# Second cross attention masked by TensorE, large stacks issued from ScalarE's queue, a new order of the streams

## The reference

```python
scores = einsum('bhqd,bhkd->bhqk', q, k) / sqrt(8)
scores = where(mask == 0, 1e-09, scores)      # X1; X0 has -inf here
attn = softmax(scores, axis=-1)
out = einsum('bhqk,bhkd->bhqd', attn, v)
return out @ WO_w.T + WO_b
```

## Time and profile before

| | |
|---|---|
| median of 3 runs | 1360.46 us (1351.87 to 1361.56) |
| profiled execution | 1365.99 us, span 1364.3 us |
| mean granted TensorE clock | 0.892 of full speed |
| busy: PE, DVE, ACT, POOL | 83%, 59%, 45%, 25% of the span |
| DMA | 58.01 MB, mean 43 GB/s |
| X1 of the lanes, round 1 | about 260 to 346 us |
| X1 of the lanes, round 2 | about 902 to 988 us |

### The profile page before, as it was taken

How to read it: one execution, slowest core, us unless ns; L and a number is a source line. 1 busy time by engine, 2 the same in 40 slices (tenths; PEclk the granted TensorE clock), 3 DMA queues, 4 the chain that set the end, 5 groups by cost and what they waited for, 6 DMA issues and landing times.

```text
span 1364.3 us, 19868 instructions
## 1 busy us (share of the span) xinstructions
PE 1133.4 (83%) x7245; PEld 648.8 (48%) x7320; DVE 811.5 (59%) x2073; ACT 618.7 (45%) x1068; POOL 342.7 (25%) x733
## 2 busy tenths in 40 slices
PE   6949567878689999969997866877869999978996
PEld 5934321443344577734465332233334467754454
DVE  3854789677873411477436379978687332169444
ACT  2116159435057543316732445844416753323852
POOL 3132210334334100124403121034334400032520
PEclk9769679779689899989978787988889999999988
DMA  7040000220600000150023200022150000042011
GB/s 251 1 109 14 0 1 1 64 55 24 172 9 2 3 0 1 45 143 3 3 62 84 54 11 0 1 55 55 57 138 3 4 1 1 1 124 65 2 34 45
DMA packets 48647, 58.01 MB, mean 43 GB/s; under 512 B 16637, under 2 KB 41645, under 8 KB 48046
## 3 DMA queue, kind: packets, MB, share of 16 engines
q1 hardware_dynamic: 47686, 56.26, 15.5%
q10 hardware_dynamic: 864, 0.48, 0.1%
HBM read 35.27 MB, written 20.87 MB: 41 GB/s over the span
## 4 chain that ended last, share of the span: by engine, by line
PE 58%; DVE 21%; issue 5%; DMA 5%; ACT 5%; POOL 4%; SPq 1%; ACTq 0%; POOLq 0%; DVEq 0%; another core or an unknown queue 0%
PE banks L1648 11%; PE banks L1658 9%; PE banks L1463 5%; PE banks L1451 5%; DVE sb_rmax L1593 4%; PE banks L1438 3%; DVE sb_arena L1383 2%; DMA sb_qs<-sb_mrows 2%; DVE sb_arena L1378 2%; PE banks L964 2%; PE banks L475 2%; PE banks L470 2%; PE banks L1264 1%; PE banks L680 1%; PE banks L1295 1%
## 5 line engine op out<-in xcount | busy, mean ns | idle before, releaser
L1593 DVE TENSOR_REDUCE sb_rmax<-banks 128x1 f32<-128x384 f32 (+3 forms) x352 | 206.5, 638 | 84.2 <-PE banks L1440 82.9
L1522 ACT ACTIVATE sb_arena<-banks 128x512 f32<-128x512 f32 x320 | 174.1, 599 | 106.0 <-PE banks L1451 82.9
L1438 PE MATMUL banks<-sb_arena,sb_qs 128*128 128x384 bf16 (+3 forms) x492 | 124.1, 324 | 42.5 <-DMA sb_arena<-k_scratch 19.3
L465 POOL TENSOR_SCALAR sb_var<-sb_mv 128x4 f32<-128x4 f32 x40 | 12.5, 311 | 570.1 <-DVE sb_mv L450 570.1
L1658 PEld LDWEIGHTS banks<-sb_w,sb_arena 128*128 128x128 f32 x1024 | 128.0, 192 | 39.9 <-issue 38.0
L1713 ACT ACTIVATE sb_arena<-banks,sb_b 128x512 f32<-128x512 f32 x128 | 84.2, 686 | 130.3 <-PE banks L1648 130.0
L1772 DVE SCALAR_TENSOR_TENSOR sb_xall<-banks,sb_region,sb_xall 128x128 f32<-128x128 f32 x160 | 44.5, 344 | 164.3 <-PE banks L1658 164.2
L1551 POOL TENSOR_SCALAR_AFFINE_SELECT sb_arena<-sb_arena 128x256 f32<-128x256 f32 x256 | 98.3, 409 | 168.0 <-ACT sb_arena L1522 167.7
L1319 ACT ACTIVATE sb_arena<-banks,sb_negmax 128x512 f32<-128x512 f32 x192 | 115.2, 714 | 42.4 <-PE banks L1264 28.3
L1648 PE MATMUL banks<-sb_ft,sb_w 128*128 128x512 f32 x256 | 129.6, 609 | 0.0
L1658 PE MATMUL banks<-sb_w,sb_arena 128*128 128x128 f32 x1024 | 129.2, 275 | 0.2 <-ACT sb_arena L1713 0.2
(11 more groups left out here) (286 smaller groups left out, 1937.8 us busy)
## 6 DMA issues: line engine op xcount, KB each, us to landing
sb_qs<-q_scratch SPq DMA_DIRECT2D x32, 288.0 KB, 5.0
q_scratch<-sb_region SPq DMA_DIRECT2D x16, 384.0 KB, 2.6
sb_arena<-k_scratch SPq DMA_DIRECT2D x16, 288.0 KB, 6.9
sb_arena<-in_chosen SPq DMA_DIRECT2D x8, 514.0 KB, 4.3
sb_w<-in_w SPq DMA_DIRECT2D x2, 2048.0 KB
q_scratch<-sb_region SPq DMA_DIRECT2D x16, 256.0 KB, 2.5
sb_qs<-q_scratch SPq DMA_DIRECT2D x32, 96.0 KB, 2.5
k_scratch<-sb_region SPq DMA_DIRECT2D x8, 384.0 KB, 2.7
```

The source lines that it names most:

```text
L1438: nc.tensor.matmul(o[:, i * kl:(i + 1) * kl], L.qs[:, h // 2, t * 128:kl], L.ks[:, key_of(h), 0:kl], start=(i == 0), stop=False)
L1522: nc.scalar.activation(L.probs[:, u % SLOTS, :], bank_of(SELF_ORDER, ring, ("key", u)), ACT.Exp)\
L1593: nc.vector.tensor_reduce(L.rmax[:, t, g * GROUP + h0:g * GROUP + h0 + nh], bank_of(SELF_ORDER, ring, ("max", step))[:, 0:nh * kl] .rearra ...
```

## The change

Four things are done.

1. X1's key scores are formed as in X0: the maximum's rows are copied into the stacked queries by SyncE (4 DMAs per X1, 16 in all, not issued before), a matmul with the identity adds -1e30 at masked keys (`shutt`), a second adds the scores. Masked keys so get weight 0. L1132 and L953 go.
2. Their share is added back at the end. TensorE sums, per query, the values (with their column of ones) of its masked keys: four fp32 matmuls per X1, of 144 columns each. VectorE copies the sums to `shut`. When all maxima are known GpSimd forms min(-max, 0) + 1e-9, ScalarE takes its exp, and GpSimd multiplies `shut` by it. `finish_tensor` adds `shut` to the spread sums by a matmul with the identity, 288 columns fp32, twice per X1.
3. The conversions of the mask (`cbias`, `maskt`, `mask`) move from X1's GpSimd stream into BU's. `shutt` is made in X1.
4. The "rest" stacks are issued from ScalarE's stream, in X0 and X1 (queries) and in S0 and S1 (queries and keys), in a piece right after the activation of queries (and keys) and before the step loop. The `ORDER` strings of all five engines are new.

```diff
-CROSS_KEY = (13, 9)
-CROSS_EXP = (13, 11)
+CROSS_KEY = (13, 13)
+CROSS_EXP = (13, 13)
...
 # cross_sync
             stack(sp, L, p, "q", L.qd, L.qs, slice(0, FIRST), "first")
-            stack(sp, L, p, "q", L.qd, L.qs, slice(FIRST, H // 2), "rest")
-            if j == 0:
-                for step in range(CROSS_STEPS):
+            for step in range(CROSS_STEPS):
...
 # cross_tensor: key_scores(h)
-                if j == 0:
-                    if h % GROUP == 0:
-                        pe.wait_ge(*p.at("mstacked", 16 * (h // GROUP + 1)))
-                    nc.tensor.matmul(o, identb[0:K2, :], L.cbiast, start=True, stop=False)
...
-            def less_maximum(h):
                 if h % GROUP == 0:
-                    pe.wait_ge(*p.at("mrows", h // GROUP + 1))
-                pe.wait_ge(*p.at("masked", h + 1))
-                nc.tensor.matmul(bank_of(order, ring, ("key", h)),
-                                 mselb[:, h % GROUP:h % GROUP + 1].to_broadcast([128, 128]),
-                                 L.mrows[:, h // GROUP % 2, :], start=False, stop=True, skip_group_check=True)\
+                    pe.wait_ge(*p.at("mstacked", 16 * (h // GROUP + 1)))
+                nc.tensor.matmul(o, identb[0:K2, :], L.shutt if j else L.cbiast, start=True, stop=False)
+                nc.tensor.matmul(o, keys_of(L, h), L.qs[:, h // 2, :], start=False, stop=True)\
                     .then_inc(L.sem("key"), 1)
...
+            if j:
+                yield
+                pe.wait_ge(*p.at("values", 1))
+                pe.wait_ge(*p.at("masks", 0))
+                for t in range(T):
+                    i = nc.tensor.matmul((b0, b3)[t // 2][:, t % 2 * H * OW:(t % 2 + 1) * H * OW],
+                                         L.maskt[:, t * 128:(t + 1) * 128], L.cvalues[:, OW:(H + 1) * OW],
+                                         start=True, stop=True)
+                i.then_inc(L.sem("summed"), 1)
 # finish_tensor, in X1
+                    if shut and two == 0:
+                        pe.wait_ge(*p.at("shut_sums", 1))
+                        nc.tensor.matmul(ring[pair][:, 0:2 * H * OW], ident[:], L.shut[:, 2 * pair:2 * pair + 2, :],
+                                         start=True, stop=False, skip_group_check=True)
 # cross_scalar
+            stack(act, L, p, "q", L.qd, L.qs, slice(FIRST, H // 2), "rest")
             for step in range(CROSS_STEPS):
...
+                if j and step == G * T + 4:
+                    yield
+                    act.wait_ge(*p.at("cut", 1))
+                    nc.scalar.activation(L.rmax[:], L.rmax[:], ACT.Exp).then_inc(L.sem("shut_exp"), 1)
 # cross_pool
-                nc.gpsimd.tensor_scalar(L.cbias[:], L.mask1, 0.0, -BIG, ALU.is_equal, ALU.mult)
-                nc.gpsimd.tensor_scalar(L.maskt[:], L.mask1t, 0.0, 0.5, ALU.is_equal, ALU.is_lt)
-                nc.gpsimd.tensor_scalar(L.mask[:], L.mask1, 0.0, None, ALU.is_equal).then_inc(L.sem("masks"), 1)
+                nc.gpsimd.tensor_scalar(L.shutt, L.maskt[:], -BIG, None, ALU.mult).then_inc(L.sem("masks"), 1)
...
+                nc.gpsimd.tensor_scalar(L.rmax[:], L.negmax[:], 0.0, 1e-9, ALU.min, ALU.add).then_inc(L.sem("cut"), 1)
                 nc.gpsimd.memset(L.ks32, 0.0).then_inc(L.sem("filled"), 1)
+                yield
+                pool.wait_ge(*p.at("shut_exp", 1))
+                pool.wait_ge(*p.at("values", 2))
+                shut = L.shut.rearrange("p t (h c) -> p t h c", c=OW)
+                nc.gpsimd.tensor_tensor(shut, shut, L.rmax[:].unsqueeze(3).to_broadcast([128, T, H, OW]), ALU.mult)\
+                    .then_inc(L.sem("shut_sums"), 1)
 # cross_vector
+                dve.wait_ge(*p.at("summed", 1))
+                for pair, bank in enumerate((b0, b3)):
+                    i = nc.vector.tensor_copy(L.shut[:, 2 * pair:2 * pair + 2, :],
+                                              bank[:, 0:2 * H * OW].rearrange("p (t n) -> p t n", t=2))
+                i.then_inc(L.sem("values"), 1)
...
-                    nc.vector.scalar_tensor_tensor(out=o, in0=o, scalar=-1e-9, in1=L.maskt[:], op0=ALU.add,
-                                                   op1=ALU.mult).then_inc(L.sem("masked"), 1)
 # bump_pool, after its memset
+            pool.wait_ge(*p.at("mask_loaded", 32))
+            nc.gpsimd.tensor_scalar(L.cbias[:], L.mask1, 0.0, -BIG, ALU.is_equal, ALU.mult)
+            nc.gpsimd.tensor_scalar(L.maskt[:], L.mask1t, 0.0, None, ALU.is_equal)
+            nc.gpsimd.tensor_scalar(L.mask[:], L.mask1, 0.0, None, ALU.is_equal).then_inc(L.sem("masks"), 1)
 # self_sync
-            for slots, done in ((slice(0, FIRST), "first"), (slice(FIRST, H // 2), "rest")):
-                stack(sp, L, p, "q", L.qd, L.qs, slots, done)
-                stack(sp, L, p, "k", L.kd, L.ks, slots, done)
+            stack(sp, L, p, "q", L.qd, L.qs, slice(0, FIRST), "first")
+            stack(sp, L, p, "k", L.kd, L.ks, slice(0, FIRST), "first")
 # self_scalar
+            stack(act, L, p, "q", L.qd, L.qs, slice(FIRST, H // 2), "rest")
+            stack(act, L, p, "k", L.kd, L.ks, slice(FIRST, H // 2), "rest")
```

More of the change, by code:

```diff
@@ L195 @@
+    "007f903bc04",
 }
@@ L570, in max_rows @@
             if g >= 2:
[L571 to L574, removed]
+                act.wait_ge(*p.at("mstacked", 16 * (g - 1)))
             nc.scalar.activation(L.mrows[0:3 * GROUP, g % 2, :], src[0:3 * GROUP, :], ACT.Copy).then_inc(L.sem("mrows"), 1)
@@ L610, in finish_tensor @@
                         i = nc.tensor.matmul(ring[pair][:, at:at + 2 * GROUP * OW], L.osb[:, two, t * 128:(t + 1) * 128],
-                                             gather[:].rearrange("p r j c -> p (r j c)"), start=True, stop=True)
+                                             gather[:].rearrange("p r j c -> p (r j c)"), start=not shut, stop=True,
+                                             skip_group_check=shut)
                 i.then_inc(L.sem("spread"), 1)
@@ L888, in cross_sync @@
             elif p.b + LANES < B:
-                sp.wait_ge(*p.last("masked"))
+                sp.wait_ge(*p.last("key"))
                 load_context(sp, L, p.b + LANES)
@@ L970, in cross_tensor @@
             pe.wait_ge(*p.at("q32", 1))
-            pe.wait_ge(*p.at("values", 1))
+            pe.wait_ge(*p.last("values"))
             pe.wait_ge(*p.at("masks", 1))
@@ L987, in cross_tensor @@
                 h = step - CROSS_KEY[j]
-                same = 1 <= h < H and order.index(("key", h)) - order.index(("key", h - 1)) == RING
-                if j and same:
-                    less_maximum(h - 1)
-                    yield
                 if 0 <= h < H:
                     key_scores(h)
-                if j and 1 <= h <= H and not same:
-                    yield
-                    less_maximum(h - 1)
                 g = cross_set(step, j)
@@ L1126, in cross_vector @@
                                                     ALU.mult, ALU.min).then_inc(L.sem("negmax"), 1)
-                h = step - CROSS_KEY[j]
-                if j and 0 <= h < H:
-                    yield
-                    dve.wait_ge(*p.at("raw", h + 1))
-                    o = bank_of(order, ring, ("key", h))[0:K2, :]
-                    nc.vector.scalar_tensor_tensor(out=o, in0=o, scalar=-1e-9, in1=L.maskt[:], op0=ALU.add,
-                                                   op1=ALU.mult).then_inc(L.sem("masked"), 1)
             yield from finish_vector(dve, L, p, ring)
@@ L1848, in _ @@
                     nc.gpsimd.memset(lane.cks32[:], 0.0)
-                    nc.gpsimd.memset(lane.mrows[:], 0.0)
                     nc.gpsimd.memset(lane.qs32[:], 0.0)
@@ L1918, in lay_out @@
         sel[part * 32:part * 32 + H] = np.eye(H)
-    msel = np.zeros((128, GROUP), np.float32)
-    for part in range(3):
-        for j in range(GROUP):
-            msel[j % 2 * 3 * GROUP // 2 + part * GROUP // 2 + j // 2, j] = 1
     gather = np.zeros((128, 2, GROUP, OW), np.float32)
```

81 lines of the change are left out of this document (40 added, 41 removed).

## The result

The changed kernel takes 1394.53 us (median of four runs, 1389.39 to 1400.75) against 1361.01 us before, measured beside it: 1.026 times the time, 95% interval 1.019 to 1.033. The forecast was 1344 us with a range up to 1370. It is some 35 us slower: the forecast was wrong in sign.

A forecast was written before the change was run, and what follows sets the result against it. TensorE was taken as busiest (83% of the span, 58% of the chain), with gains possible only in attention stages. The terms -9 - 3 - 7 - 2 + 3 + 2 = -16 us from 1360.5 gave 1344 us, range 1320 to 1370.

The forecast's parts named there:

- Order of stacks: At 16 stage starts, large query stacks may now start before keys are parked, sharing with small stacks: -2 us, ends +40, -27.
- my rival of 1350 us: Both queues share the same DMA engines: row transfers gain only 3 us, order of stacks nothing; 1350 us, chance 0.10.
- ScalarE pays: ScalarE's 48 stack issues and its in-order wait for park completions, in X and S stages: +3 us.
- The slower rival: ScalarE, waiting in order for parks, blocks the other lane's exponentials or Gelus; six holds give 1376 us, chance 0.17.
- Large stacks from ScalarE's queue: Maximum's rows no longer queue behind the other lane's large stacks, so TensorE waits less: -7 us, ends 0 and -10.
- The mask pass and its preparation: VectorE's mask pass in X1 goes, -9 us; mask conversions move from X1 into BU, -3 us.
- +2 for additions: In X1, added fp32 matmuls of 1.5 us at start and 1.5 at end; +2 us, ends 0 and +12.
- 0 for the order: The new order strings of all engines follow costs that cannot be seen: 0 us, ends -8 and +8.
- given back: VectorE's relief in attention becomes waits for TensorE and row DMAs, so mask terms are 0: 1357 us, chance 0.18.
- VectorE was the limit: Half of the mask pass's 43.2 us comes off, -22, and earlier stacks give 10: 1323 us, chance 0.17.
- The company that I feared in BU: Mask conversions now run in BU beside VectorE's 2048-wide operations and could slow them: nothing taken, end of +10 us.

The follow-up runs named there:

- e1_sp_all: The changed kernel with every large stack issued by SyncE again, right behind the small ones; 1348.69 us, 0.994 of the kernel before.
- e3_wait_only: e1_sp_all, with ScalarE waiting for the parks where the changed kernel issued stacks, but issuing nothing; 1349.02 us, 0.995 of the kernel before.
- e7_after_kpark: The changed kernel, with ScalarE in self attentions issuing the large query stack only after the key park has landed too; 1368.54 us, ratio 1.009.
- e5_after_small: The changed kernel, with ScalarE issuing the large stacks only after the small stacks have landed; 1366.57 us, 1.008 of the kernel before.
- e9_hold_small: e5_after_small with its ScalarE waits kept, but the large stacks issued by SyncE as in e1_sp_all; 1357.31 us, 1.003 of the kernel before.
- e10_before_row: The kernel before, with only the first maximum-row transfer of three attention stages (not X1) issued from ScalarE's queue; 1353.31 us, ratio 0.998.
- e6_row_act: e1_sp_all, with the first maximum-row transfer (12 KB) of each stage issued from ScalarE's queue; 1337.18 us, 0.987 of the kernel before.
- e8_traffic: e3_wait_only, plus two unread 288 KB DRAM-to-DRAM transfers in ScalarE's queue behind each of its waits; 1381.62 us, 1.020 of the kernel before.

## Why the prediction was wrong

**The step that failed** is "Order of stacks". Its ends were +40 and -27 and I took -2, "for the transfers fill a gap in which the queue waited for the parks". No run has this term by itself. Putting the large stacks into ScalarE's queue holds three terms of the sum, -7, -2 and +3, together -6; measured they are +43, give or take 10 (the changed kernel against e1_sp_all). The wait for parks of normal length was free (e3_wait_only) and the rows' idle time did fall, so the loss lies in this term, at or past its bad end. The gap in SyncE's queue was no gap of the DMA engines: it is the time in which the parks fly, and the next thing to fly is the small stack for which TensorE waits. The row that gave the bad end was the earlier trace rows: small stacks 2.5 us when alone in front. The changed kernel's issues by size:

```profile
sb_qs<-q_scratch ACTq DMA_DIRECT2D x32, 288.0 KB, 5.1
...
sb_qs<-q_scratch SPq DMA_DIRECT2D x32, 96.0 KB, 5.3
...
sb_arena<-k_scratch SPq DMA_DIRECT2D x16, 96.0 KB, 4.3
...
k_scratch<-sb_region SPq DMA_DIRECT2D x8, 128.0 KB, 5.4
```

and those of e1_sp_all:

```profile
sb_qs<-q_scratch SPq DMA_DIRECT2D x32, 288.0 KB, 4.7
...
sb_qs<-q_scratch SPq DMA_DIRECT2D x32, 96.0 KB, 2.5
...
sb_arena<-k_scratch SPq DMA_DIRECT2D x16, 96.0 KB, 2.2
...
k_scratch<-sb_region SPq DMA_DIRECT2D x8, 128.0 KB, 2.8
```

96 KB now take as long as 288 KB. I had priced 2.5 us at each of 16 starts; by these rows an S start pays it about twice (2.6 for the last key park, 2.1 for the small key stack), an X start 2.8 once; that the park pays as well is what the term left out. I also counted no park among the delayed transfers, and they are about half of it: freeing the key parks gave back 23 us of the 43 (e7_after_kpark). Foreign bytes cost 34 us at the same places, in part by other waits.

The Trainium skill's "DMA: Bandwidth & Descriptors", the section on issuing engines not being separate queues, says that DMAs of all engines interleave on the same 16. The runs agree (small query stacks took 5.3 us with two queues loaded, 2.5 with one), and with more than I let it say: I used it to shrink a gain (my rival of 1350 us), where interleaving has a price as well as no benefit. Its section on queues and completion order, by which an engine alternates between queues at packet boundaries, would let a small transfer pass a large one in part. The runs show little of that: the small query stacks landed in 5.3 us where each of the large ones beside them, three times as many bytes, took 5.1.

**ScalarE pays:** +3 was taken. The wait as such costs nothing measurable while parks are short (e3_wait_only against e1_sp_all, 0.995 and 0.994). The slower rival, 1376 us by six full holds, had the right sign, but its cause is not the main one: e5_after_small holds ScalarE's L573 longer (43.5 us in place of 31.4) and is 25 us faster than the changed kernel. A hold one transfer longer costs 11 us (e9_hold_small), so the mechanism exists; what part it has in the changed kernel, where the parks themselves grew, stays open.

**Large stacks from ScalarE's queue:** -7 was taken for the row transfers. TensorE's idle time for them fell from 12.2 us (7.7 at L1438, and 2.8 and 1.7 at two more lines) to 4.4: -7.8. As idle time this term was right, though two row transfers in its chain still took 4.37 and 4.42 us where none was to take over 4. What it is worth in time no run tells by itself: 7.7 us less of the same idle time gave e10_before_row 3 us, 10.1 less gave e6_row_act 10, and that by moving 12 KB instead of 576 (X) or 1152 (S) a stage. One step of its working was misread: rows that land 4.2 us sooner make up for less than the 4.58 us stalled, not more.

**The mask pass and its preparation:** -9 and -3, +2 for additions, 0 for the order, -10 together. e1_sp_all has -7.6 (0.3 to 0.9%), with X1's new row transfers queued behind large stacks; e10_before_row to e6_row_act gives -15. The sum was about right, with the new order in both figures. VectorE's busy time fell by 36.0 us in e1_sp_all (39 forecast). The timeline of VectorE in e1_sp_all from the query split to the residual, both lanes' first X1, answers to the earlier trace rows:

```profile
264.63 0.83 DVE L482 CAST sb_region<-sb_q 128x512 bf16<-128x512 f32 x1
288.37 0.43 DVE L482 CAST sb_region<-sb_q 128x512 bf16<-128x512 f32 x1
324.51 0.69 DVE L1139 TENSOR_TENSOR sb_xall<-banks,sb_nrm 128x512 f32<-128x512 f32 x1 [2.38 <-PE banks L476]
...
345.38 0.69 DVE L1139 TENSOR_TENSOR sb_xall<-banks,sb_nrm 128x512 f32<-128x512 f32 x1 [2.46 <-PE banks L476]
```

The second lane's X1 takes 57.0 us where it took 62.7, less than X0 of before (61.2): X0 was no yardstick for it, and the rival "given back" took its 1.5 us from there. From the first split to the last residual this pair of X1 takes 80.8 us in place of 86.2, the second pair 84.3 in place of 86.2; some 6 a pair were forecast. 8 to 15 us in all are well short of the 22 that "VectorE was the limit" gave the mask pass alone. The company that I feared in BU does not show: its 2048-wide operations take 1383 ns in the mean in the changed kernel and took 1396. The longest query cast is 843 ns in place of the earlier trace rows's 1606; no run shows what made that one. The added matmuls cost what was estimated, in e1_sp_all:

```profile
L607 PE MATMUL banks<-sb_region,sb_ident 128*128 128x288 f32 x16 | 5.4, 418 | 0.0
L961 PE MATMUL banks<-sb_cvalues,sb_maskt 77*128 77x144 f32 x32 | 5.2, 307 | 0.0
```

1.35 and 1.3 us per X1, for 1.5 and 1.5.

## What to carry to other kernels

Before moving a large transfer to a second queue, list what flies in the interval into which it moves, and count every transfer there for which the path waits, the parks included; here each took about twice as long (2.8 to 5.4 us, 2.5 to 5.3, 2.2 to 4.3). Move the small, late, urgent transfer to the free queue and leave the large ones behind the work that the path waits for. A wait placed in an engine's stream was free up to the parks and cost 11 us one transfer later, so read what stands behind it. And an experiment that reproduces most of a loss may do so along another path: compare its waits with the original's before calling the cause shown.

## What the runs showed of the hardware

- Large transfers in a second queue slowed small ones in the first: 96 KB of queries landed in 5.3 us beside large stacks, in 3.9 beside foreign transfers of 288 KB, in 2.5 with one queue. What flies beside matters as well as how much: the last key park took 5.4 us beside the large stacks and 2.8 beside the foreign ones. The time lost was nearly in proportion to the foreign bytes (18 us for half, 34 for all).
- How much two loaded queues moved depended on the transfers: 243 and 164 GB/s at the first start of a self attention in the changed kernel, 291 and 227 there in e8_traffic. No run carries the same transfers at the same time by one queue and by two.
- A transfer of 12 KB alone in ScalarE's queue, issued beside SyncE's large stacks, could still take as long as one queued behind them. The chain of e6_row_act has one with 7.08 us and one with 5.89, where e1_sp_all has four of 5.57 to 7.04:

```profile
588.62 7.08 DMA sb_qs<-sb_mrows
...
1204.55 5.89 DMA sb_qs<-sb_mrows
```

- A DMA stall is paid for twice. The changed kernel and e1_sp_all have the same 7368 matmuls, in 1141.8 and 1128.9 us. Of the 51.1 us between their spans 35.8 are TensorE's longer idle time for stacks, less its shorter one for rows (48.5 - 12.7), and 12.9 are the same matmuls run slower. The granted clock fell from 0.94 to 0.50 in the stall from 588.20 us, in which TensorE did nothing, and its mean over the span is 0.878 against 0.905.
